# A graph network's gate, norm and dense stage as one pipeline over pairs, a third buffer in the node sums, row numbers by ScalarE

## What is computed

```python
norm = edge_weight * rsqrt(deg_out[src] * deg_in[dst] + EPS)                    # layer 0, twice:
h = relu(segment_sum((h @ W)[src] * norm, dst) + b)
chn_se = x * sigmoid(relu(mean(x) @ w1 + b1) @ w2 + b2)                         # layer 1
spa = sigmoid(segment_sum((x @ gcn_w)[src] * (dis[src] * dis[dst]), dst) + gcn_b)
x = layernorm(x + (x * spa + x + chn_se))
msgs = silu(concatenate([x[row], x[col]]) @ W1.T + b1) @ W2.T + b2              # layer 2
agg = segment_sum(msgs, row) / (cnt + 1e-08)                                    # then a GRU cell
y = concatenate([segment_sum((x @ W_f.T)[row] * ew, col), segment_sum((x @ W_b.T)[col] * ew, row)]) + bias
```

## Time and profile before

| | us |
|---|---|
| median of 3 runs | 7823.03 (7819.34 to 7823.38) |
| profiled execution, its own time | 7812.24 |
| its span | 7810.3 |
| PE busy | 5506.7 (71%) |
| DVE busy | 4777.8 (61%) |
| POOL busy | 4482.2 (57%) |
| ACT busy | 1767.0 (23%) |

### The profile page before, as it was taken

How to read it: one execution, slowest core, us unless ns; L and a number is a source line. 1 busy time by engine, 2 the same in 40 slices (tenths; PEclk the granted TensorE clock), 3 DMA queues, 4 the chain that set the end, 5 groups by cost and what they waited for, 6 DMA issues and landing times. The chain is left out here.

```text
span 7810.3 us, 131476 instructions
## 1 busy us (share of the span) xinstructions
PE 5506.7 (71%) x23656; PEld 3597.3 (46%) x23657; DVE 4777.8 (61%) x13613; ACT 1767.0 (23%) x2560; POOL 4482.2 (57%) x5046
## 2 busy tenths in 40 slices
PE   5566667799999887379999979915555555555550
PEld 4333334467777556355555545504333333333330
DVE  8878777467777766657777755464333333343335
ACT  4100000168888520023333323300000000000000
POOL 0377777467777710017777740004777777777770
PEclk7577778799999985589999999956555555555555
DMA  2244444343333303133333350012111123111122
GB/s 89 50 125 125 122 125 130 99 134 103 103 103 103 100 19 93 43 116 104 104 104 103 104 109 0 0 43 57 52 52 52 52 51 51 52 52 52 52 50 64
DMA packets 317648, 612.92 MB, mean 78 GB/s; under 512 B 90563, under 2 KB 177804, under 8 KB 317130
## 3 DMA queue, kind: packets, MB, share of 16 engines
q0 software_dynamic: 185408, 469.86, 22.7%
q1 hardware_dynamic: 132106, 141.78, 6.0%
HBM read 573.87 MB, written 43.84 MB: 79 GB/s over the span
## 5 line engine op out<-in xcount | busy, mean ns | idle before, releaser
L1601 DVE TENSOR_TENSOR acc<-bank,acc 128x256 f32 (+1 forms) x3552 | 1271.8, 358 | 1710.4 <-PE bank L760 1347.8
L760 PE MATMUL bank<-ring,oh 128*128 128x128 f32 x3552 | 1337.4, 485 | 932.7 <-issue 622.2
L760 PEld LDWEIGHTS bank<-ring,oh 128*128 128x128 f32 x3552 | 885.8, 312 | 1384.5 <-issue 989.9
L535 POOL DMA_INDIRECT ring<-h_table,stage_i x888 | 857.2, 965 | 255.8 <-PE bank L833 152.0
L535 POOL DMA_INDIRECT ring<-fwd_table,stage_i x888 | 846.3, 953 | 261.1 <-issue 195.9
L535 POOL DMA_INDIRECT ring<-q_table,stage_i x888 | 845.4, 952 | 262.6 <-issue 145.5
L535 POOL DMA_INDIRECT ring<-bwd_table,stage_i x888 | 845.7, 952 | 258.9 <-issue 179.9
L1161 ACT ACTIVATE ring<-big 128x889 f16<-128x889 f16 x840 | 874.1, 1041 | 213.8 <-PE bank L844 182.5
L520 POOL CAST stage_i<-s_idx 128x8 int32 (+1 forms) x224 | 46.4, 207 | 1440.1 <-issue 727.6
L844 PE MATMUL bank<-ring,big 128*128 128x445 f16 (+1 forms) x3360 | 773.9, 352 | 0.0
L1612 DVE TENSOR_SCALAR oh<-iota,d_loc,d_norm 128x128 f32<-128x128 f32 x1776 | 651.9, 370 | 70.2 <-DVE big L1685 20.3
(11 more groups left out here) (384 smaller groups left out, 7592.7 us busy)
## 6 DMA issues: line engine op xcount, KB each, us to landing
big<-places_in_block SPq DMA_DIRECT2D x111, 256.0 KB
acc<-places_in_block SPq DMA_DIRECT2D x74, 384.0 KB
ring<-h_table,stage_i POOLq DMA_INDIRECT x888, 2.8
ring<-q_table,stage_i POOLq DMA_INDIRECT x888, 2.8
ring<-fwd_table,stage_i POOLq DMA_INDIRECT x888, 2.5
ring<-bwd_table,stage_i POOLq DMA_INDIRECT x888, 2.5
big<-x_and_degree,stage_i POOLq DMA_INDIRECT x536, 2.8
h_table<-hq SPq DMA_DIRECT2D x50, 128.0 KB, 1.7
```

The source lines that it names most:

```text
L535: pool.indirect_dma_start(out=gbuf[:, u % RING, 0:width], out_offset=None, in_=table, in_offset=bass.IndirectOffsetOnAxis(ap=stage_i[:, v, ...
L760: pe.matmul(bank[u % 4][:, 0:width], oh[:, u % 4, :], gbuf[:, u % RING, 0:width], start=True, stop=True).then_inc(S["mm"], 1)
L1601: dve.tensor_tensor(to, bank[u % 4][:, 0:width], to, ALU.add).then_inc(S["accd"], 1)
```

## The change

- **Row numbers.** ACT makes the conversions into `stage_i`, ahead of time, at chosen places of its own stream: in pass 1 behind each root; in pass 2 between sign rows; in pass 3 behind every second group's silu; in passes 4 and 5 in loops of their own. Except in passes 1 and 3, where an earlier wait covers it, ACT first waits for `mm`. POOL's streams hold only gathers. Before pass 1 POOL converts five octets and issues 40 gathers (36 before). An activation of type Sqrt stands ahead of two of ACT's loops.
- **Node sums.** Three buffers, in loops of three batches; `select_slots(b)` waits for the sums of b-3.
- **One pipeline over pairs.** `staggered` runs turns t = 0, 1, ...; in turn t each engine works on pairs t, t-1, ... as below, from the last pair down. `p3` is laid out by block, so that a finished pair's parts overwrite rows no longer needed. The normalised pair goes to `x2_buf`, which PE turns directly and SP stores. ACT makes the first two parts of `p3`, DVE the difference and the third. POOL clears `acc` after the node sums.

```diff
+def staggered(engine, turns, lag, step):
+    for t in range(lag):
+        step(t, t % 2)
+    twice = (turns - lag) // 2
+    with engine.Fori(0, twice) as i:
+        for k in range(2):
+            step(i * 2 + lag + k, (lag + k) % 2)
+    for t in range(lag + 2 * twice, turns + lag):
+        step(t, t % 2)
...
-            def gathers(k, table, width, index, free, base, together=1):
...
-                        if u % RING == RING // 2 - 1:
-                            stage(i * SPAN + RING * (v + 1), (v + 1) % 3)
...
+            pool.wait_ge(S["spa_in"], 1)
+            pool.memset(acc_flat, 0.0).then_inc(S["acc_clear"], 1)
...
+                with pe.Fori(0, BATCHES // 3) as i:
+                    for k in range(3):
+                        slot_values(i * 3 + 2 + k, (2 + k) % 3)
+                        slot_sums(i * 3 + 1 + k, (1 + k) % 3)
+                slot_sums(BATCHES - 1, 1)
...
+            def d4_turn(t, par):
+                i, k2 = t - 3, (par + 1) % 2
+                if in_range(i, PAIRS):
+                    pe.wait_ge(S["x2_done"], i + 1)
+                    pe.wait_ge(S["d_at"], i * 2 + 2 * NBE)
                     for q in range(2):
-                        n = i * 2 + q + 2 * NBE
-                        pe.wait_ge(pair["p_in"][q], BASE["p_in"] + i * 16 + 16)
-                        pe.wait_ge(S["d_at"], n + 1)
-                        turn(n, q, staged_x[:, q, :], 4 + q)
-                if first:
-                    return
-                for q in range(2):
-                    n = i * 2 - 2 + q
-                    pe.wait_ge(S["d_at"], n + 1 + 2 + 2 * NBE)
-                    pe.wait_ge(S["d_h"], n + 1 + NBE)
-                    pe.wait_ge(S["p_split"], n + 1)
-                    for k in range(2):
-                        pe.matmul(bank[2 + q][:, 0:D], turned[:, q, k * P:(k + 1) * P], w_ab[:, k, D:2 * D], start=(k == 0), stop=(k == 1))
-                    for k in range(2):
-                        pe.matmul(bank[6 + q][:, 0:D], turned[:, q, k * P:(k + 1) * P], w_ab[:, k, 0:D], start=(k == 0), stop=False)
-                    pe.matmul(bank[6 + q][:, 0:D], ones_b[:, :], bias_parts[:, D:2 * D], start=False, stop=True).then_inc(S["d_m"], 1)
-            in_turns(pe, PAIRS, d4_products, 1)
+                        for k in range(2):
+                            mm = pe.transpose(bank[4 + k2][:, k * D + q * P:k * D + (q + 1) * P],
+                                              x2_buf[k2][:, q * D + k * P:q * D + (k + 1) * P], ident[:, :])
+                    mm.then_inc(S["d_t"], 2)
+                i, k2 = t - 4, par
+                if in_range(i, PAIRS):
+                    pe.wait_ge(S["d_at"], i * 2 + 4 + 2 * NBE)
+                    pe.wait_ge(S["p_diff"], i + 1)
+                    pe.wait_ge(S["d_h"], i * 2 + NBE)
+                    for q in range(2):
+                        for k in range(2):
+                            pe.matmul(bank[6 + k2][:, q * D:(q + 1) * D], turned[:, k2, k * D + q * P:k * D + (q + 1) * P], w_ab[:, k, 0:D], start=(k == 0), stop=False)
+                        pe.matmul(bank[6 + k2][:, q * D:(q + 1) * D], ones_b[:, :], bias_parts[:, D:2 * D], start=False, stop=True)
+                    for q in range(2):
+                        for k in range(2):
+                            mm = pe.matmul(bank[2 + k2][:, q * D:(q + 1) * D], turned[:, k2, k * D + q * P:k * D + (q + 1) * P], w_ab[:, k, D:2 * D], start=(k == 0), stop=(k == 1))
+                    mm.then_inc(S["d_m"], 2)
+            staggered(pe, PAIRS, 4, d4_turn)
...
+            def stage(index, first, v):
+                act.activation(stage_i[:, v, :], index[:, ds(first, RING)], ACT.Copy).then_inc(S["staged"], 1)
...
+            def stage_again(octet, slot, index, pass_no):
+                act.wait_ge(S["mm"], octet * RING + T * pass_no - 2 * RING + 8)
+                stage(index, octet * RING, slot)
...
+            def d4_functions(t, par):
+                last = countdown(act, t, PAIRS)
+                i, k2 = t - 2, par
+                if in_range(i, PAIRS):
+                    act.wait_ge(S["x2_agg"], i + 1)
+                    act.activation(std_k[k2].rearrange("p q a -> p (q a)"), mv_k[k2][:, :, 1:2].rearrange("p q a -> p (q a)"), ACT.Sqrt,
+                                   bias=cols[:, 10:11]).then_inc(S["x2_std"], 1)
+                i, k2 = t - 3, (par + 1) % 2
+                if in_range(i, PAIRS):
+                    act.wait_ge(S["d_t"], i * 2 + 4 + 2 * NBE)
+                    act.wait_ge(S["d_m"], i * 2 + 2 * NBE)
+                    act.activation(turned[:, k2, :], bank[4 + k2][:, :], ACT.Copy).then_inc(S["d_at"], 2)
+                i, k2 = t - 4, par
+                if in_range(i, PAIRS):
+                    n = last + 8
+                    act.wait_ge(S["d_m"], i * 2 + 4 + 2 * NBE)
+                    act.activation(p3[:, 0, ds(n, 2), :], bank[6 + k2][:, :].rearrange("p (q f) -> p q f", q=2), ACT.Copy).then_inc(S["p_high"], 1)
+                    if not (isinstance(i, int) and i == 0):
+                        for q in range(2):
+                            act.wait_ge(pair["tab_out"][q], BASE["tab_out"] + i * 16)
+                    act.activation(hq[:, :, :], bank[2 + k2][:, :].rearrange("p (q f) -> p q f", q=2), ACT.Copy).then_inc(S["d_h"], 2)
+                i = t - 5
+                if in_range(i, PAIRS):
+                    n = last + 10
+                    act.wait_ge(S["p_diff"], i + 1 + 2)
+                    act.activation(p3[:, 1, ds(n, 2), :], rest_p.rearrange("p (q f) -> p q f", q=2), ACT.Copy).then_inc(S["p_mid"], 1)
+            act.activation(cols[:, 12:13], half_less[:, 0:1], ACT.Sqrt)
+            staggered(act, PAIRS, 5, d4_functions)
...
+            def select_slots(b, k, turn):
+                dve.wait_ge(rows_in[k], turn * 16 + LOADED[k] + 16)
                 dve.wait_ge(S["slot_val"], b + 1)
                 dve.tensor_scalar(slot_oh[:, k, :], slot_rows[:, k, :], node_no[:, :], None, ALU.is_equal).then_inc(S["slot_sel"], 1)
...
+            def d4_turn(t, par):
+                last = countdown(dve, t, PAIRS)
+                both_of = lambda s, n: p3[:, s, ds(n, 2), :]
+                by_block = lambda a: a.rearrange("p (q f) -> p q f", q=2)
+                i = t - 3
+                if in_range(i, PAIRS):
+                    dve.wait_ge(S["x2_std"], i + 1)
+                    inverse = std_k[(par + 1) % 2].rearrange("p q a -> p (q a)")
+                    dve.reciprocal(inverse, inverse).then_inc(S["x2_inv"], 1)
+                i = t - 6
+                if in_range(i, PAIRS):
+                    dve.wait_ge(S["p_mid"], i + 1)
+                    dve.tensor_tensor(both_of(2, last + 12), by_block(rest_p), both_of(1, last + 12), ALU.subtract).then_inc(S["p_split"], 1)
+                i = t - 5
+                if in_range(i, PAIRS):
+                    dve.wait_ge(S["p_high"], i + 1)
+                    if not (isinstance(i, int) and i == 0):
+                        dve.wait_ge(S["p_split"], i)
+                    dve.tensor_tensor(by_block(rest_p), by_block(bank[6 + (par + 1) % 2][:, :]), both_of(0, last + 10), ALU.subtract).then_inc(S["p_diff"], 1)
+                i = t - 3
+                if in_range(i, PAIRS):
+                    dve.wait_ge(S["x2_inv"], i + 1)
+                    dve.wait_ge(S["d_t"], i * 2 + 2 * NBE)
+                    if not (isinstance(i, int) and i < 2):
+                        dve.wait_ge(S["x2_out"], i * 16 - 16)
+                    for q in range(2):
+                        n = last + 6 + q
+                        o = dve.tensor_scalar(x2_buf[(par + 1) % 2][:, q * D:(q + 1) * D], x_of(n), mv_k[(par + 1) % 2][:, q, 0:1], std_k[(par + 1) % 2][:, q, :], ALU.subtract, ALU.mult)
+                    o.then_inc(S["x2_done"], 1)
+                i = t
+                if in_range(i, PAIRS):
+                    for q in range(2):
+                        n = last + q
+                        o = dve.scalar_tensor_tensor(x_of(n), gate_bc[:, :], sm["spa"][:, ds(n, 1)], x_of(n), ALU.add, ALU.mult)
+                    o.then_inc(S["x2_mul"], 1)
+                i = t - 2
+                if in_range(i, PAIRS):
+                    dve.wait_ge(S["x2_stat"], i + 1)
+                    apart(dve, S["waited"])
+                    for q in range(2):
+                        o = dve.bn_aggr(mv_k[par][:, q, :], stats_k[par][:, q, :])
+                    o.then_inc(S["x2_agg"], 1)
+                i = t - 1
+                if in_range(i, PAIRS):
+                    dve.wait_ge(S["x2_mul"], i + 1)
+                    for q in range(2):
+                        n = last + 2 + q
+                        o = dve.bn_stats(stats_k[(par + 1) % 2][:, q, :], x_of(n))
+                    o.then_inc(S["x2_stat"], 1)
+            staggered(dve, PAIRS, 6, d4_turn)
+            dve.wait_ge(S["p_split"], PAIRS)
+            dve.wait_ge(S["acc_clear"], 2)
```

(61 more changed lines are left out.)

217 lines of the change are left out of this document (99 added, 118 removed).

## The result

The changed kernel takes 7758.61 us in the median (7750.53 to 7762.77, four runs), the kernel before 7823.2 (7819.34 to 7823.44, four): a ratio of 0.9917, with a 95% interval of 0.99 to 0.9935. The forecast of 7736 was 22.6 us too low and its range of 7675 to 7795 held. The profiled execution after takes 7762.77 us with a span of 7760.8. It is the slowest of its four, and the profiled execution of before (7812.24) is faster than all four of its own, so that the spans are 49.5 us apart and the medians 64.6. What follows compares the spans.

The account below looks back on a forecast made before the run. POOL's back-to-back gathers were taken to bound the passes, a chain of waits the node sums, PE the dense loop. Row numbers -43, node sums -82 and gate to dense stage +38 gave -87 us: median 7736, range 7675 to 7795.

Parts of the forecast that it names:

- the ring of waits in the dense stage: Gate to dense stage: products wait through ACT's copies, DVE's parts and norm, and PE's transposes; one set per 12.0 us round.
- the pace of the node sums: Node sums: with a third buffer only the work is left, PE setting 3.15 us a batch instead of 4.26; -82 us.
- the sum: Whole kernel: row numbers -43, node sums -82, gate to dense stage +38, together -87 us against the profiled 7812.24.
- of such a stretch at half clock I take 5 us to fall on PE's work: Gate to dense stage: after each 4.5 us gap, slow clock loses 2.5 us, making rounds 12.0 us instead of 9.5.
- rival 2: Gate to dense stage: PE's clock never recovers, rounds of 14.5 us, 7794 us in all; chance 0.09.
- bound of 357: Gate to dense stage: upper bound in us, with rounds of 14.5 us wholly at half clock; +96 us.
- POOL is some 30 tiles ahead and may be 40: Pass 1: without conversions POOL can gain only 10 tiles of lead, 13 us; 12 taken with the tail, less DVE's bursts.
- Rival 3: Node sums gain less, PE's own queue making 3.43 us a batch: 7757 us; chance 0.12 for its full case and conversions worthless.
- Rival 4: Passes: row numbers from ACT come late at an octet's first gather, slower than before, 8013 us if 0.5 us late; chance 0.06.
- Rival 5: Passes: POOL's conversions were never worth a thing, 43 us less gain, 7779 us; chance 0.12 shared with smaller node-sum gains.
- Rival 1: Gate to dense stage: the clock holds, rounds of 9.5 us, stage 19 us shorter, 7679 us in all; chance 0.17.

Follow-up runs that it names:

- the filler: The changed kernel with six more fp32 matmuls that nothing reads, queued on PE behind the products of each pair: 7669.37 us, one run.

## Why the prediction was right, and where its sizes were off

Direction and range held, and the ring of waits in the dense stage and the pace of the node sums were the predicted ones. The clock within the ring and POOL's lead in pass 1 were not. The forecast for the profiled execution was -87 us; the spans fell by 49.5. The 37.5 us between them are the sum of five differences, and that the median lies even in the forecast's own range of 7700 to 7770 is in part luck: 28.3, 10.4 and 10.8 us one way meet 8.5 and 3.5 the other.

- **Gate to dense stage, +66.3 where the sum had +38: 28.3 us off, the largest error.** The ring was right, step by step: products, three copies, third part, difference, norm, transposes; PE idle for 4.45 us against 4.5. The mis-sized term is the clock's, "of such a stretch at half clock I take 5 us to fall on PE's work". All of it falls there: 13.63 - 4.45 = 9.2 us of work at half clock a round, where the sum had 4.99 + 2.5. The row I took it from was of a pass in which PE resumed and kept working; here PE stops just as the clock rises, and full speed is spent on the idle piece. It rose some 9 us after PE had resumed, where the row had 5.7; why, no run shows. So the state is rival 2's (0.50 during PE's work, 0.65 over the stage where the prediction had 0.75), at a round of 13.6 us instead of its 14.5. The stage stayed 29 us under its bound of 357, because 13.6 is less than 14.5 and because the first two rounds (11.3 and 12.6 us between PE's starts) and the last three (10.2) are shorter. A rule of the Trainium skill (TensorE: Matmul & The Clock Gate, "HAM oscillation") says as much, that such a loop starts every group of matmuls slow. The trace agrees (0.50 for 9 of the 9.2 us), and so does the filler, which had 1.00 with gaps of 1.87 us.
- **Pass 1, -1.6 where the sum had -12.** The step that failed is "POOL is some 30 tiles ahead and may be 40". The groups from 355 to 1250 us show the lead; those of the gathers of before are the first row and this one:

```profile
L561 POOL DMA_INDIRECT ring<-x_and_degree,stage_i x271 | 270.5, 998 | 77.7 <-issue 53.3 <-PE bank L793 20.4 <-POOL stage_i L546 4.0
```

and those of after, with PE's products under them:

```profile
L587 POOL DMA_INDIRECT big<-x_and_degree,stage_i x392 | 405.5, 1034 | 153.5 <-issue 79.8 <-PE bank L816 73.7
L587 POOL DMA_INDIRECT ring<-x_and_degree,stage_i x268 | 277.0, 1034 | 81.7 <-issue 51.8 <-PE bank L816 29.9
...
L816 PE MATMUL bank<-big,oh 128*128 128x256 f32 x796 | 342.4, 564 | 186.6 <-DVE oh L1725 182.1
L816 PE MATMUL bank<-ring,oh 128*128 128x256 f32 x544 | 209.1, 513 | 70.4 <-DVE oh L1725 66.1 <-DVE acc L1714 0.9
```

  Two products are one tile. By 1250 us POOL has issued 36 + 396 + 271 = 703 gathers before and 40 + 392 + 268 = 700 after. PE has done 1344 / 2 = 672 tiles before (L793, x800 and x544 over the same stretch) and 1340 / 2 = 670 after. The lead is 31 and 30: a POOL with less to do was no further ahead. And this is near the low end. When POOL starts gathers 80, 120 and 200, PE has done 42, 82 and 162 tiles in both kernels, a lead of 38 in a ring of 40. The ten tiles that the prediction meant to gain were not there. DVE waits for no gather from 370 to 1250 us in either kernel; as the prediction had it, DVE and PE set the pace there, 1.34 us a gather in both.

  Where POOL's time went can be counted, and it is not into waits for a free place. PE is named for 44.8 us of POOL's idle time before and for 103.6 after, but 31.7 of these are one wait ahead of the 41st gather (before, POOL stood 35.5 us for DVE at a conversion there), 2.1 are another, and nearly all the others are the gap of 0.3 us between any two gathers. The conversions took 31.9 us. In their place each gather takes 1.034 us in the mean instead of 1.003, and the gap 0.31 instead of 0.29. Why the gathers get longer, no run shows. What is left of the gain is the tail, 1.27 us a gather before and 1.26 after, over 185.
- **Passes 2 to 5, -34.5 where the sum had -31.** Right, by the rows of gathers. The octet of pass 4 shown above takes 0.05 us less; in the mean of the four passes it is 34.5 / 444 = 0.08.
- **Node sums, -90.5 where the sum had -82.** 219.3 / 74 = 2.96 us a batch, not 3.15. PE paces the stage, as foreseen. The mis-sized term is PE's work, which the prediction took from the busy time of 232.15 us. By line, PE's two groups take 124.3 and 112.9 us before and 124.1 and 110.9 after, so their work is nearly the same. But 2.8 of the 232.15 us belong to seven matmuls ahead of the node sums, and the records of neighbouring groups overlap: by 7.8 us in sum before, by some 15 after, where no gap parts them. Rival 3 falls, and the buffers alone, without the rest of the change, give the same length.
- **Not in the sum, +10.8.** The first gather starts 3.8 us later, the stretches between the stages take 0.4, 2.6 and 2.7 us more and the end 1.8, less 0.5 between passes 4 and 5. Of the dense stage's 66.3, 5.9 are DVE's first norm under POOL's clearing. The prediction laid the clearing beside the pipeline at no cost; it cost more than half of its own length, and with the shorter rounds that its later place brought, 17 us.

Rival 4 is refuted on the first chip: one wait of 0.3 us in pass 2 and none in passes 3 to 5. Rival 5 falls with the 34.5 us. Rival 1 was reached only by the filler kernel: 9.37 us a round at clock 1.00, a stage of 245.1 us against its 242.

The gain that the new pipeline was able to give was there all the time: with the norm queued ahead of the parts the stage is 104 us shorter than before instead of 66 longer.

## What to carry to other kernels

In a software pipeline with one turn per engine, follow the chain from each engine's first wait around until it comes back: if it passes through every engine once a round, the pipeline does one step at a time, however deep its lags are, and what feeds the bound engine is to be queued ahead of what empties behind it, in one queue. Price an idle piece of PE at what the clock loses as well, and look in windows of a single round at which part of it gets the full clock. Before pricing a faster producer, count its lead from tiles issued and consumed: where the ring is as good as full it has nothing to give.

## What the hardware showed that I had not expected

- **DVE's first norm takes 6.3 us instead of 0.41** (6.62 for the two) and ends at 3142.29, 0.15 us behind the end of POOL's clearing at 3142.14. DVE's gate and statistics (L1997, L2013) ran beside the same clearing at their usual length (medians 0.48 and 0.40 us), and a subtraction of two rows beside the later one at 0.69. A rule of the Trainium skill sorts these cases (SBUF — State Buffer, "SBUF: two separate sides"): GpSimd and VectorE share a pair of ports that is locked for a whole instruction by whoever comes first, and VectorE wants it in a two-port mode, or with two inputs from SBUF if GpSimd's instruction reads SBUF. The clearing only writes. The rows agree, if the norm, with one tensor from SBUF, runs in that mode and the statistics don't; neither was tried.
- **The granted clock rises while PE stands still.** In the windows above 1.00 falls on the idle piece, and the 17 rounds between the norms at 3168.20 and 3399.84 are all 13.6 us long: the two phases lock, and PE hardly sees the higher clock.
- **PE at 98% busy keeps 0.50 through the node sums**, 223 us, and the fp32 products of the dense stage, with idle pieces of 0.3 to 1.9 us between them, have 1.00. Why, no run shows.
- **Two other chips are slow in the passes alone.** Node sums (219.1 and 309.4 us) and gate to dense stage (261.7 in the kernel with the node sums alone, as 261.5 before) agree to 0.3 us with the first chip, while passes 2 to 5 take 1334 to 1825 us instead of 1114 to 1135. In these, PE and DVE stop for 2 to 8 us at a time, often together, with a releaser (what ended the wait) that the profile calls remote or does not name. POOL gathers on until its ring is full and then waits for them. The waits of DVE and POOL in pass 3 on chip 3, with the node sums alone changed, from 4400 to 4800 us:

```profile
POOL ring L538 <- DVE ring L1907: 160.7, 29, 7.1
DVE oh L1887 <- remote: 160.5, 24, 7.6
```

  The cause stays open. The lesson does not: the edit that saves POOL's time gains 34.5 us on one chip and loses 23 to 32 on the two others, and what was gained in a stage without gathers is the same on all three.
